# A hybrid of Mamba, linear attention and experts: dt bounded in PSUM's copy, u one chunk earlier on POOL

## What is computed

```python
x_conv = jax.nn.silu(xc.swapaxes(1, 2))
delta = jax.nn.softplus(x_conv @ dt_proj_w.T + dt_proj_b)
delta = jnp.clip(delta, 0.0001, 10.0)
A = -jnp.exp(A_log)
# per step of the scan, 512 channels x 16 states
dA = jnp.exp(jnp.clip(dt[..., None] * A, -10.0, 0.0))
dBx = dt[..., None] * bt[:, None, :] * xt[..., None]
h = dA * h + dBx
# every 16th step h is scaled down to a norm of at most 10 per channel
y = jnp.einsum('bn,ben->be', ct, h) + D_param * xt
```

## Time and profile before

| | us |
|---|---|
| median of 3 runs | 4514.08 (4511.81 to 4515.91) |
| the profiled execution | 4514.84 |
| its span in the trace | 4512.8 |
| PE, DVE, ACT, POOL busy in the span | 4253.3, 3632.4, 3057.9, 2588.5 |
| granted TensorE clock, mean | 0.987 |

### The profile page before, as it was taken

How to read it: one execution, slowest core, us unless ns; L and a number is a source line. 1 busy time by engine, 2 the same in 40 slices (tenths; PEclk the granted TensorE clock), 3 DMA queues, 4 the chain that set the end, 5 groups by cost and what they waited for, 6 DMA issues and landing times.

```text
span 4512.8 us, 79944 instructions
## 1 busy us (share of the span) xinstructions
PE 4253.3 (94%) x22592; PEld 2960.7 (66%) x22592; DVE 3632.4 (80%) x9610; ACT 3057.9 (68%) x8912; POOL 2588.5 (57%) x1284
## 2 busy tenths in 40 slices
PE   5899999999999999999999999988999999999999
PEld 4777777777777777777777777644444444444444
DVE  3899999999999999999999999855656657566666
ACT  5898888888888888888888888834333332333321
POOL 3988888888888888888888888930000000000000
PEclk8999999999999999999999999999999999999999
DMA  2111111111111111111111111100000000000000
GB/s 101 58 51 62 49 58 53 57 54 57 54 57 54 57 54 57 54 57 54 56 53 54 54 56 55 55 30 22 6 16 16 6 16 6 16 16 7 6 7 10
DMA packets 91560, 187.49 MB, mean 42 GB/s; under 512 B 16160, under 2 KB 58016, under 8 KB 90912
## 3 DMA queue, kind: packets, MB, share of 16 engines
q1 hardware_dynamic: 90272, 180.78, 12.2%
q10 hardware_dynamic: 1152, 5.14, 0.3%
HBM read 168.05 MB, written 17.83 MB: 41 GB/s over the span
## 4 chain that ended last, share of the span: by engine, by line
PE 49%; issue 19%; DVE 18%; POOL 11%; ACT 2%; DVEq 1%; POOLq 0%; DMA 0%; SPq 0%; ACTq 0%
PE ps L684 24%; POOL prod L331 6%; DVE macc L1004 6%; PE ps L658 4%; PE ps L808 3%; POOL hb L339 3%; PE ps L736 2%; PE ps L730 2%; PE ps L750 2%; PE ps L773 2%; PE ps L790 2%; POOL xcv L355 1%; DVE dtt L1189 1%; PE ps_dA L808 1%; PE ps L758 1%
## 5 line engine op out<-in xcount | busy, mean ns | idle before, releaser
L684 PE MATMUL ps<-w_x,mxT 128*128 128x512 f32 x4096 | 1933.7, 601 | 69.6 <-DVE macc L1004 69.6
L1004 DVE SCALAR_TENSOR_TENSOR macc<-ps,gate,macc 128x256 f32<-128x256 f32 x2048 | 977.6, 477 | 498.0 <-PE ps L684 410.0
L915 DVE TENSOR_TENSOR_SCAN hb<-ps_dA,hb 128x1088 f32<-128x1088 f32 x512 | 1240.7, 2423 | 107.4 <-POOL hb L339 99.1
L331 POOL TENSOR_TENSOR prod<-hb,cbc 128x1024 f32<-128x1024 f32 x512 | 1123.1, 2194 | 248.9 <-DVE hb L934 243.5
L339 POOL TENSOR_TENSOR hb<-u,bbc 128x1024 f32<-128x1024 f32 x512 | 1202.0, 2348 | 75.1 <-POOL prod L331 70.9
L394 ACT ACTIVATE zr<-dt,aneg 128x128 f32<-128x128 f32 x4096 | 1240.8, 388 | 1.3 <-DVE dt L1078 1.0
L684 PEld LDWEIGHTS ps<-w_x,mxT 128*128 128x128 f32 x4096 | 727.5, 191 | 739.3 <-issue 604.0
L658 PEld LDWEIGHTS ps<-prod,ident 128*128 128x128 f32 x8192 | 947.5, 192 | 151.9 <-POOL prod L331 91.4
L658 PE MATMUL ps<-prod,ident 128*128 128x128 f32 x8192 | 965.4, 276 | 41.0 <-POOL prod L331 41.0
L403 ACT ACTIVATE ps_dA<-zr 128x1024 f32<-128x1024 f32 x512 | 518.3, 1012 | 0.0
L410 ACT ACTIVATE sq<-hb 128x64 f32<-128x64 f32 x512 | 157.9, 308 | 219.9 <-DVE hb L915 217.4
(11 more groups left out here) (193 smaller groups left out, 4848.3 us busy)
## 6 DMA issues: line engine op xcount, KB each, us to landing
bbc<-bcd SPq DMA_DIRECT2D x128, 512.0 KB, 3.8
cbc<-bcd SPq DMA_DIRECT2D x128, 512.0 KB, 3.7
xt<-in_x SPq DMA_DIRECT2D x128, 128.0 KB, 3.6
x2d<-macc SPq DMA_DIRECT2D x64, 128.0 KB, 1.7
out_dram<-macc SPq DMA_DIRECT2D x64, 128.0 KB, 1.7
w_x<-in_w_x ACTq DMA_DIRECT2D x1, 4096.0 KB, 12.6
hb<-x2d SPq DMA_DIRECT2D x32, 128.0 KB, 2.4
sz<-x2d SPq DMA_DIRECT2D x16, 128.0 KB, 2.2
```

The lines of the kernel that those rows point to most:

```text
L331: TT(dst, states, cc, ALU.mult).then_inc(M["prodp"], 1)
L684: last = mm(banks[p % len(banks)][:], mxT[k][:, j, :], w_x[:, j, p * 512:(p + 1) * 512], start=(j == 0), stop=(j == KD - 1))
L915: V.tensor_tensor_scan(states, dA, states, 0.0, ALU.mult, ALU.add).then_inc(M["scan"], 1)
L1004: STT(macc[k][:], banks[(e // 2) % len(banks)][:, (e % 2) * D:(e % 2 + 1) * D], gate[k][:, e:e + 1], macc[k][:], ALU.mult, ALU.add).then_i ...
```

## The change

DVE no longer adds dt's bias: it bounds the raw projection between dt_lo and dt_hi, two columns per channel block computed once from b_dt. ACT adds the bias in its Exp, one instruction per block since the bias is per channel, and writes Ln's result into dt. The TENSOR_SCALAR of chunk 0 is gone with its waits; those who waited for it wait for ACT's Ln. Ln now waits until u has read the dt before. POOL does u in chunk 0, before product(0) and inputs(2), in place of chunk 1, behind them.

```diff
--- before.py
+++ after.py
@@ -84,6 +84,7 @@
         sz = [sb(f"sz{k}", [P, EB, P]) for k in range(2)]
         xcv = [sb(f"xcv{k}", [P, EB, P]) for k in range(2)]
         dt = sb("dt", [P, EB, P])
+        dt_hi, dt_lo = (sb(n, [P, EB]) for n in ("dt_hi", "dt_lo"))
         dtt = sb("dtt", [P, EB, P])
         dcw = sb("dcw", [P, EB * TAPS, P])
         ddp = sb("ddp", [P, EB, P])
@@ -155,7 +156,7 @@
         s_w, s_setup, s_aexp, s_zero = sig("s_w"), sig("s_setup"), sig("s_aexp"), sig("s_zero")
         s_settle, s_passed = sig("s_settle"), sig("s_passed")
 
-        dve_m = ("st1", "mv1", "vp", "den", "sx1", "nx", "keep", "xib", "zb", "xcc", "bcv", "dtb", "dt", "scan", "nr",
+        dve_m = ("st1", "mv1", "vp", "den", "sx1", "nx", "keep", "xib", "zb", "xcc", "bcv", "dtb", "scan", "nr",
                  "st0", "hs", "yg", "o1", "o2", "st3", "mv3", "vc3", "se3", "r3", "o3", "o4")
         act_m = ("xn", "carry", "lnp", "r1", "qs", "xnTs", "ez", "lz", "ss", "ex", "lx", "sx", "edt", "ldt", "zr", "dA", "sq", "nl",
                  "ne", "ln3", "sd3")
@@ -342,8 +343,8 @@
                    .broadcast_to([P, EB, N, CH]), ALU.mult).then_inc(M["bt"], 1)
 
             def extra(i, k, c, stages):
-                if c == 1 and "G" in stages:
-                    g.wait_ge(M["dt"], AHEAD + i + 2)
+                if c == 0 and "G" in stages:
+                    g.wait_ge(M["ldt"], AHEAD + i + 2)
                     g.wait_ge(M["xcv"], AHEAD + i + 2)
                     TT(u[1 - k][:], dt[:], xcv[1 - k][:], ALU.mult).then_inc(M["u"], 1)
                 if c == 4 and "G" in stages:
@@ -388,7 +389,7 @@
             def decays(i, k, lo, hi):
 
                 if lo == 0:
-                    a.wait_ge(M["dt"], AHEAD + i + 1)
+                    a.wait_ge(M["ldt"], AHEAD + i + 1)
                     a.wait_ge(M["dA"], AHEAD + (i - 1) * NC)
                 for s in range(lo, hi):
                     last = act(zr[k][:, s, :], dt[:, s // N, :], ACT.Relu, bias=10.0, scale=aneg[:, s:s + 1])
@@ -545,9 +546,12 @@
                     if c == 7:
                         if F:
                             a.wait_ge(M["dtb"], AHEAD + (i + 3) * EB)
-                            act(dtt[:], dtt[:], ACT.Exp).then_inc(M["edt"], 1)
+                            for e in range(EB):
+                                last = act(dtt[:, e, :], dtt[:, e, :], ACT.Exp, bias=b_dt[:, e:e + 1])
+                            last.then_inc(M["edt"], 1)
                             a.wait_ge(M["edt"], AHEAD + i + 3)
-                            act(dtt[:], dtt[:], ACT.Ln, bias=1.0).then_inc(M["ldt"], 1)
+                            a.wait_ge(M["u"], AHEAD + (i + 2 if G_ else 0))
+                            act(dt[:], dtt[:], ACT.Ln, bias=1.0).then_inc(M["ldt"], 1)
                         if X_:
                             route_init(i - 2, k, x1b[k][:], lambda: a.wait_ge(R["o"][k], AHEAD + (i - 2 - k) * 8))
                     if G_ and DECAYS[c] < DECAYS[c + 1]:
@@ -1071,11 +1075,6 @@
                 if X_:
                     v.wait_ge(M["x1"], AHEAD + i - 1)
                     route_norm1(i - 2, x1b[k][:])
-                if G_:
-                    v.wait_ge(M["ldt"], AHEAD + i + 2)
-                    v.wait_ge(M["zr"], AHEAD + i + 1)
-                    v.wait_ge(M["u"], AHEAD + i + 1)
-                    TS(dt[:], dtt[:], 1e-4, 10.0, ALU.max, ALU.min).then_inc(M["dt"], 1)
                 if B:
                     v.wait_ge(M["xr"], AHEAD + i * 16)
                     v.wait_ge(M["x1"], AHEAD + i - 1)
@@ -1184,9 +1183,9 @@
                 halfway(7)
                 if F:
                     v.wait_ge(M["dtp"], AHEAD + i + 3)
-                    v.wait_ge(M["dt"], AHEAD + (i + 2 if G_ else 0))
+                    v.wait_ge(M["ldt"], AHEAD + (i + 2 if G_ else 0))
                     for e in range(EB):
-                        TS(dtt[:, e, :], F0[:, e * P:(e + 1) * P], b_dt[:, e:e + 1], 40.0, ALU.add, ALU.min)\
+                        TS(dtt[:, e, :], F0[:, e * P:(e + 1) * P], dt_hi[:, e:e + 1], dt_lo[:, e:e + 1], ALU.min, ALU.max)\
                             .then_inc(M["dtb"], 1)
                 router(10, 11)
                 if X_:
@@ -1197,6 +1196,8 @@
                 n = dst.shape[1]
                 TT(dst[:], ident[:].rearrange("p (a c) -> p a c", a=1).broadcast_to([P, n, P]),
                    w.rearrange("p (a c) -> p a c", c=1).broadcast_to([P, n, P]), ALU.mult).then_inc(s_zero, 1)
+            for bound_of, x in ((dt_hi, 10.0), (dt_lo, 1e-4)):
+                TS(bound_of[:], b_dt[:], -1.0, math.log(math.expm1(x)), ALU.mult, ALU.add)
             V.memset(hb[0][:, :, 0:1], 0.0)
             V.memset(xin[:], 0.0)
             V.memset(carry[:, 0:NT // 2 - 1], 1.0)
```

## The result

The changed kernel takes 4626.39 us (median of 4 runs, 4623.43 to 4628.11), the kernel before, run beside it, 4514.05: a ratio of 1.0248, 95% interval 1.0231 to 1.0266. It is slower by 112 us, where 35 us less was forecast, and it lies above the range of 4464 to 4541. Without one cause that has nothing to do with the operations that were changed, it takes 4510 us, and that number was in the forecast, as rival B. The experiments take the two apart.

What follows compares the result with a forecast made beforehand. No engine clearly bound; DVE and POOL pace each other in a ring, PE nearly full. Per tile 0.80 - 0.30 = 0.50, 0.20 more in the other kind, mean 0.60, less 0.05; 0.55 x 64 = 35 us: 4479, range 4464 to 4541.

Steps and rivals of the forecast that it cites:

- rival B: Chunk 0: u wins the tie in every second tile, which loses about 0.4; the other gains 0.55; 4509, chance 0.20.
- A: Both kinds of tile gain, u late by 0.1 to 0.4: 4479, own range 4464 to 4492, chance 0.52.
- I take L1082 first, since it asks first: Chunk 0, where u and L1082 want to start together: DVE's L1082 goes first and u is held by 0.30.
- A's sum: Per tile 0.80 - 0.30 = 0.50 gained in one kind, about 0.20 more in the other.
- u held by 0.30: Chunk 0 on POOL: u waits 0.30 for L1082, at least 0 and at most 0.47.
- The two pointers: DVE's L1189 with two pointers: 0.24 per tile at most, 0.24 taken, hidden by L994's wait of 0.28 for POOL.
- The four Exps: ACT: one Exp of 630 ns becomes four, 0.92 more at most, hidden in ACT's idle of 1.30 before the next squares.
- the step for chunks 4 to 7: In chunk 4 DVE's L1140 follows PE's conv, so DVE's lead can't exceed PE's 0.40; 0.05 per tile taken off.
- the 0.5 that the prediction named as a sign of being wrong: A new DVE idle of over 0.5 before L1140 would show the prediction wrong.
- DVE's wait for POOL was to fall to about 35 in 48 tiles: Sign of being right: scan(3) no longer waits for POOL, DVE's wait falling from 72.0 to about 35 us.
- Rival C: Slower: L1082 waits behind u in every tile, 0.83 late; 0.4 per tile lost, 4539, chance 0.18.
- D: Nothing moves, because PE at 97% paces after all: 4514, chance 0.05.

Runs made afterwards that it cites:

- e1: The changed kernel with 9 semaphore increments more on DVE and 84 on ACT ahead of the pipeline, nothing inside the loop touched: 4509.91 us, ratio 0.9987.
- e11: e1 with L1084 one instruction earlier on DVE, ahead of the small TENSOR_SCALAR of the router's mean: 4480.02 us, ratio 0.9921.
- e9: The whole change without L1084, PE adding the output's bias row as one more product, 20 increments ahead of DVE's loop: 4473.39 us, ratio 0.991.
- e10: e9 with u back in POOL's chunk 1: 4471.29 us, ratio 0.9908.
- e7: e1 without L1084, PE adding the output's bias row as one more product, 12 increments ahead of DVE's loop: 4675.16 us, ratio 1.035.

## Why the prediction was wrong

**The step that failed** is that the change's cost was worked out from durations alone. The two setup operations were put at "under 1 us once" and L1078 with its waits at what it takes in the timeline; nothing asked where the loop's code lies. The change takes 9 of DVE's records from ahead of the loop and 4 from a pass. That moves the loop from record 574 to 565. Its start is then at a place where DVE stands for 3.8 us at the branch of every pass; a pass takes 4.3 us more, 2.7 by the stall itself and 1.6 in mean by the lower granted clock behind it. That makes 116 us, over three times what the whole change was to bring. The granted clock, 1.00 in the earlier trace rows, was silently kept at that. The row that could have warned stood in the view of waits of before: DVE's scan waits 0.20 for issue once per pass, so there is a branch on DVE's path, and the page has a count of instruction packets. That this kernel's pass of 373 had only 12 places in 128 to lie in, nothing in the old profile shows.

**The choice between A and B** failed too, and would have by itself: without the stall the change takes 4509.91, B's mechanism and B's number (4509). A had 0.52 and B 0.20. B's two prices per tile were 0.55 gained and 0.4 lost, measured 0.54 and 0.42; it had L1082 0.72 late, and in e1 it ends 0.73 late (6.24 us after the start of the tile's first scan, where it was 5.51). The numbers for the tie, 1073.30 and 1073.29, were in the earlier trace rows; "I take L1082 first, since it asks first" holds where it asks clearly first; in that kind of tile it asked only 0.01 us before u's start, and that wasn't enough.

**What held.** A's sum (0.50 in one kind and 0.20 more in the other) is what e11 measures once DVE asks first in both: 0.54 and 0.72, 4480.02 against the forecast 4479. The path is a little different: scan(3) waits for POOL no longer (0.80), but scan(2) now does (0.55 or 0.56 in e11's timeline), since product(0) and inputs(2) are behind u. u held by 0.30: measured 0.18 by its length, L1082 ending 0.28 or 0.29 behind POOL's instruction. The two pointers: 0.24 per tile, taken and measured; in e1 L994's wait is gone (0.17 long in place of the 0.45 of the earlier trace rows) and pays for it: from the norm's reduce to the next tile's scan(0) DVE takes 2.27, where it took 2.30. The four Exps take 1.28 in place of 0.63, 0.65 more under the bound of 0.92, and squares(0) still finds ACT idle. L1140 waits for conv, as the step for chunks 4 to 7 had it: 0.28 in e1's first kind of tile and 0.93 in the other, over the 0.5 that the prediction named as a sign of being wrong, and 0.34 to 0.41 in e11. DVE's wait for POOL was to fall to about 35 in 48 tiles: 26.8 in e1, where the second kind doesn't wait at all since u's win delays DVE, and 49.1 in e11.

**Rival C** (u first in every tile) is excluded by the first kind, where a waiting DVE goes first. **D** (PE paces) is excluded for this change by e11; e9 and e10 show where it begins.

## What to carry to other kernels

In a kernel with a loop, every edit to an engine's program moves that loop's code, even one made only outside of it. Moving the loop's start by 9 records was worth 116 us here. Compare the packets of the instruction queues and each engine's wait for "issue" before and after, first of all, and if they rose, shift the loop with a few idle instructions until they fall before judging the edit itself. Read what such a stall costs from whole passes and not from the idle time of the engine that stands: here it was less (2.7 for 3.8), and the lower TensorE clock behind it came on top. And where a DVE operation and a POOL operation are to start within some hundredths of each other, put one clearly ahead: the order of two neighbouring instructions decided 30 us here.

## What was new in the hardware's behaviour

- A loop of 369 DVE instructions is kept or fetched again depending on where it starts. Fetching costs DVE 3.8 us of idle at the branch (7.3 in e7) and about 5 packets of 8.2 KB per engine and pass: (216 - 81) / 28 = 4.8.
- Behind such a stall of DVE the granted TensorE clock fell to its lower level in 24 of 27 passes of the changed kernel, after PE had stood four times for 0.5 to 2.0 us. A pass at 0.98 took 1.8 us more than one at 1.00 with the same stall (95.36 and 93.56).
- The same on ACT, 2.1 us per pass, cost nothing, although ACT is 90% busy.
- Between DVE and POOL a DVE operation that asked 0.31 us or more before POOL's next instruction started went first, one that asked 0.01 to 0.03 before it didn't. The loser waits until the other has ended: L1084 took 1.56 behind u, u 1.45 in place of 1.27 behind L1084.
- A TENSOR_SCALAR of 128x128 from PSUM takes 402 ns with two pointer operands and 341 with one.
